# Two-layer attention kernel on one core: four instead of three of the first batch's tiles mixed by ScalarE with TensorE, and the second batch's mixing spread otherwise over GpSimd's queue

## What is computed

```python
x = L0_attn_x                       # [2, 1024, 512]
xn = _layernorm(x)
x = x + attention0(xn) + mix0(xn)   # one head, d = 128; mix0 below
xn = _layernorm(x)
x = x + attention1(xn) + ffn1(xn)   # 32 heads on 8 latent key/value heads, causal; LoRA with top-2 of 8 experts

def mix0(x):                        # a row is seen as 4 streams of 128
    H_res = sinkhorn_log(logits_res, 50)      # 4x4 per row
    H_res = (1 - g) * I + g * H_res
    x_pre = einsum('btnc,btn->btc', x_streams, H_pre)
    y = x_pre @ W_branch
    x_mixed = einsum('btij,btjc->btic', H_res, x_streams)
    return x_mixed + einsum('btc,btn->btnc', y, H_post)
```

## Time and profile before

| what | value |
|---|---|
| median of 3 runs | 2352.6 us (2350.76 to 2353.61) |
| the profiled execution's own time | 2355.71 us |
| its span, first to last instruction | 2353.9 us |
| mean granted TensorE clock | 0.981 of full |
| busy share PE, DVE, ACT, POOL | 95%, 66%, 45%, 43% |
| `layer0_mix` | from about 84.4 to 232.5 us of the span |
| attention of the first batch | from about 352 to 1290 us |

### The profile page before, as it was taken

The page is one execution under the profiler, slowest core; times in us unless marked ns, Lnnn a source line. Parts: engine busy times, 40 slices in busy tenths (PEclk is TensorE's granted clock), DMA queues, the critical chain, the costliest instruction groups (busy, mean ns, idle before and its releaser), DMA issues. The chain is left out here.

```text
span 2353.9 us, 34666 instructions
## 1 busy us (share of the span) xinstructions
PE 2235.7 (95%) x11190; PEld 1817.0 (77%) x11190; DVE 1543.9 (66%) x3818; ACT 1070.3 (45%) x2282; POOL 1017.1 (43%) x1124
## 2 busy tenths in 40 slices
PE   6898999999999999989998898999999999999998
PEld 5554778888888888778777677888888888888886
DVE  6778566777777776746555474656566666666565
ACT  2555334544545454535344232545454545454454
POOL 5331714453536263857654011525344444434341
PEclk9999999999999999999999999999999999999999
DMA  9600582010110101020010464010101010101000
GB/s 339 216 1 17 215 300 81 11 61 27 45 36 36 54 18 54 24 64 24 17 48 6 173 251 152 28 52 20 62 9 62 9 62 9 62 9 62 27 32 32
DMA packets 74168, 165.26 MB, mean 70 GB/s; under 512 B 4721, under 2 KB 38897, under 8 KB 67442
## 3 DMA queue, kind: packets, MB, share of 16 engines
q1 hardware_dynamic: 73650, 162.95, 19.7%
q10 hardware_dynamic: 432, 1.32, 0.1%
HBM read 113.40 MB, written 72.61 MB: 79 GB/s over the span
## 5 line engine op out<-in xcount | busy, mean ns | idle before, releaser
L1868 DVE TENSOR_TENSOR pT<-psum,pT 128x512 fp32r<-128x512 f32 x576 | 387.4, 689 | 265.0 <-ACT pT L1916 262.5
L1768 POOL TENSOR_TENSOR probs_even<-probs_even,rinv 128x1024 f32<-128x1024 f32 (+2 forms) x192 | 241.1, 1256 | 564.0 <-DVE rinv L1859 564.0
L1916 ACT ACTIVATE pT<-psum 128x512 fp32r<-128x512 f32 x576 | 331.5, 597 | 319.3 <-PE psum L1977 319.1
L1854 DVE CUSTOM_DVE_ANT_0 psum<-psum,causal 128x256 f32<-128x256 f32 (+7 forms) x512 | 385.9, 767 | 54.2 <-PE psum L98 50.2
L1907 ACT ACTIVATE probs_even<-psum,nmax 128x1024 f32<-128x1024 f32 (+3 forms) x256 | 204.4, 799 | 263.9 <-DVE nmax L1854 260.5
L1768 POOL TENSOR_TENSOR probs_odd<-probs_odd,rinv 128x896 f32<-128x896 f32 (+2 forms) x192 | 198.8, 1043 | 270.0 <-DVE rinv L1859 269.8
L96 PE MATMUL psum<-keys,q 128*128 128x512 f32 (+3 forms) x768 | 267.9, 349 | 15.3 <-DMA keys<-k_parts 11.6
L97 PE MATMUL psum<-keys,q 128*128 128x512 f32 (+3 forms) x768 | 263.7, 343 | 0.0
L98 PE MATMUL psum<-keys,q 128*128 128x512 f32 (+3 forms) x768 | 263.5, 343 | 0.0
L96 PE MATMUL psum<-pT,vals 128*128 128x512 f32 x576 | 256.4, 445 | 4.5 <-DVE pT L1868 0.7
L1907 ACT ACTIVATE probs_odd<-psum,nmax 128x896 f32<-128x896 f32 (+3 forms) x256 | 176.6, 691 | 146.3 <-DVE nmax L1854 143.5
(11 more groups left out here) (304 smaller groups left out, 4444.6 us busy)
## 6 DMA issues: line engine op xcount, KB each, us to landing
wq<-wq_copy SPq DMA_DIRECT2D x16, 1024.0 KB, 4.8
k_parts<-kv_out SPq DMA_DIRECT2D x32, 512.0 KB, 3.7
v_parts<-kv_out SPq DMA_DIRECT2D x32, 512.0 KB, 3.7
wo<-wo_copy SPq DMA_DIRECT2D x16, 1024.0 KB, 4.8
keys<-k_parts SPq DMA_DIRECT2D x32, 512.0 KB, 4.8
vals<-v_parts SPq DMA_DIRECT2D x64, 256.0 KB, 3.2
acc<-in_x SPq DMA_DIRECT2D x4, 1024.0 KB, 11.8
xn_later<-xn SPq DMA_DIRECT2D x1, 2048.0 KB, 14.5
```

The costliest lines, as they stand in the source:

```text
L1768: pool.tensor_tensor(p, p, rinv[:, u, h:h + 1].to_broadcast([P, (TB - u) * P]), ALU.mult).then_inc(p_ok, 1)
L1854: dve.tensor_tensor_reduce(out=row, in0=row, in1=causal[:, S - n:S], scale=-1.0, scalar=-2 * MASKED, op0=ALU.add, op1=ALU.min, accum_out=n ...
L1868: dve.tensor_tensor(pT[:, n % PT_SLOTS, 1, :], bank[T_BANK + n % 2], f32(pT[:, n % PT_SLOTS, 0, :]), ALU.subtract).then_inc(t_lo, 1)
L1916: act.activation(pT[:, n % PT_SLOTS, 0, :], bank[T_BANK + n % 2], ACT.Copy).then_inc(t_hi, 1)
```

## The change

In `layer0_mix` tile 4 goes from VectorE to the products (15 become 20), and its bias from GpSimd to the bias matmul. The last unit's `branch_in`, `turn_xp`, `branch` and `take_y` go from the attention's loop to the products (behind products 3 and 5 on TensorE, 5 and 7 on ScalarE), in bank 5. The heads' copy `oT` goes ahead of the exponential of the unit's last tile. Nobody waits any more in that stage for the store of y; ScalarE's first write over y's place in `layer1_inputs` and SP's first `later_loads` do. In the first batch's attention the second batch's tiles go 2, 3, 3 instead of 3, 3, 2 to the iterations 5, 6 and 7, with steps per norm of their own for each, and SP's loads of tiles stand at other places. The diff, cut to its core:

```diff
@@ layer0_project, gpsimd
             add_bo(3)
-            add_bo(4)
@@ layer0_mix
-        BY_ACT, SHARE_SLOTS = range(TB - 3, TB), 8
+        BY_ACT, SHARE_SLOTS = range(TB - 4, TB), 8
@@ sync
-            sp.dma_start(m.y_s, y[:, TB:NT, :]).then_inc(later, 16)
-            sp.wait_ge(later, 32)
+            sp.dma_start(m.y_s, y[:, TB:NT, :]).then_inc(m.y_stored, 16)
+            sp.wait_ge(later, 16)
@@ vector
-            for tiles in ((0, 1), (2, 3, 4)):
+            for tiles in ((0, 1), (2, 3)):
@@ scalar (turn_xp, take_y read bank 5 for the last unit)
-                        if qt == 0:
+                        if qt == 0 and unit < UNITS:
                             take_y(unit - 1)
...
+                        if qt == UQ - 1:
+                            act.wait_ge(pv_mm, TB * unit)
+                            act.activation(oT[:], bank[6][:], ACT.Copy).then_inc(o_ok, 1)
                     if unit < UNITS:
                         t = UQ * unit + qt
...
-                if unit:
-                    act.wait_ge(pv_mm, TB * unit)
-                    act.activation(oT[:], bank[6][:], ACT.Copy).then_inc(o_ok, 1)
-                if unit < UNITS:
+                if unit < UNITS - 1:
                     turn_xp(unit)
             for e in range(TB // 2, (NS + 1) * len(BY_ACT)):
                 product(e)
+                if e == TB // 2 + 1:
+                    turn_xp(UNITS - 1)
+                if e == TB // 2 + 3:
+                    take_y(UNITS - 1)
@@ tensor
-                            branch(unit - 1)
+                            if unit < UNITS:
+                                branch(unit - 1)
...
-                if unit < UNITS:
+                if unit < UNITS - 1:
                     branch_in(unit)
...
+                    if e == TB // 2:
+                        branch_in(UNITS - 1)
+                    if e == TB // 2 + 2:
+                        branch(UNITS - 1)
+                    if n == 3 and j == 0:
+                        pe.wait_ge(y_ok, UNITS)
@@ layer1_inputs, scalar
+            if first:
+                act.wait_ge(m.y_stored, 16)
             high_latent(0)
@@ layer1_attention
-            tiles_of = {5: (0, 1, 2), 6: (3, 4, 5), 7: (6, 7)}
-            mixing_steps = {2: (1, 1, 3), 4: (1, 1, 2), 5: (1, 1, 1), 7: (0, 0, 3)}
+            tiles_of = {5: (0, 1), 6: (2, 3, 4), 7: (5, 6, 7)}
+            spread = {0: (1, 1, 1), 2: (1, 1, 1), 4: (1, 1, 1), 5: (1, 1, 1), 7: (0, 0, 3)}
+            mixing_steps = {5: {2: (1, 1, 1), 4: (1, 1, 1), 5: (1, 1, 0), 7: (0, 0, 2)}, 6: spread,
+                            7: {0: (1, 1, 1), 2: (1, 1, 2), 3: (1, 1, 2), 4: (1, 1, 2)}}
@@ sync, loads
-                for t in mixed_now[:2]:
+                for t in mixed_now[:1]:
                     later_loads(t + 1)
...
-                for t in mixed_now[2:]:
+                for t in mixed_now[1:-1]:
                     later_loads(t + 1)
...
                 load(wo[:, 1], m.wo_s[g]).then_inc(wo_in, 16)
+                for t in mixed_now[-1:]:
+                    later_loads(t + 1)
```

More of the change, by code:

```diff
@@ L727, in turn_xp @@
                 act.wait_ge(xp_mm, n + 1)
[L728 removed]
+                act.activation(y[:, UQ * n:UQ * n + UQ, :].rearrange("p t d -> p (t d)"), bank[0 if n < UNITS - 1 else 5][:], ACT.Copy).then_inc(xpT_ok, 1)
             def take_y(n):
                 act.wait_ge(y_mm, n + 1)
[L732 removed]
+                act.activation(y[:, UQ * n:UQ * n + UQ, :].rearrange("p t d -> p (t d)"), bank[1 if n < UNITS - 1 else 5][:], ACT.Copy).then_inc(y_ok, 1)
             def product(e):
@@ L799, in branch_in @@
                     for j in range(NS):
-                        last = pe.matmul(bank[0][:, k * P:(k + 1) * P], shares[:, k, j, :], m.ident[:], start=j == 0, stop=j == NS - 1)
+                        last = pe.matmul(bank[0 if n < UNITS - 1 else 5][:, k * P:(k + 1) * P], shares[:, k, j, :], m.ident[:], start=j == 0, stop=j == NS - 1)
                 last.then_inc(xp_mm, 1)
@@ L805, in branch @@
                 for k in range(UQ):
-                    last = pe.matmul(bank[1][:, k * P:(k + 1) * P], y[:, UQ * n + k, :], wbr[:], start=True, stop=True)
+                    last = pe.matmul(bank[1 if n < UNITS - 1 else 5][:, k * P:(k + 1) * P], y[:, UQ * n + k, :], wbr[:], start=True, stop=True)
                 last.then_inc(y_mm, 1)
@@ L841, in _ @@
                                 pe.wait_ge(w_in, 48)
-                            branch(unit - 1)
+                            if unit < UNITS:
+                                branch(unit - 1)
                             pe.wait_ge(p_exp, UQ * unit)
                             turn(0)
-                            pe.wait_ge(y_ok, unit)
+                            pe.wait_ge(y_ok, min(unit, UNITS - 1))
                             turn(1)
@@ L1712, in _ @@
             if mixes_later:
+                sp.wait_ge(m.y_stored, 16)
                 later_loads(0)
@@ L1716, in _ @@
             if mixes_later:
-                later_loads(TB - 1)
+                for t in tiles_of[ITERS - 1][:-1]:
+                    later_loads(t + 1)
             for u in range(TB):
@@ L1768, in body @@
                         pool.tensor_tensor(p, p, rinv[:, u, h:h + 1].to_broadcast([P, (TB - u) * P]), ALU.mult).then_inc(p_ok, 1)
-                        if mixes_later and it >= mixing_from and u in mixing_steps:
-                            for _ in range(mixing_steps[u][h]):
+                        if mixes_later and it >= mixing_from and u in mixing_steps[it]:
+                            for _ in range(mixing_steps[it][u][h]):
                                 next(beside, None)
@@ L2057, in program @@
         m.xn_s, m.y_s = internal("xn_later", (P, TB, HID)), internal("y_later", (P, TB, D))
-        m.ffn_in, m.ffn_hi, m.copied = (ctx.enter_context(nc.semaphore(n)) for n in ("ffn_in", "ffn_hi", "copied"))
+        m.ffn_in, m.ffn_hi, m.copied, m.y_stored = (ctx.enter_context(nc.semaphore(n)) for n in ("ffn_in", "ffn_hi", "copied", "y_stored"))
         m.w_hi, m.wq_in, m.wq_ok, m.wo_in = ([ctx.enter_context(nc.semaphore(f"{n}{b}")) for b in range(B)]
```

## The result

| kernel | median, us | runs | ratio to before |
|---|---|---|---|
| before | 2352.8 | 4 (2350.8 to 2353.6) | |
| changed | 2328.6 | 4 (2326.8 to 2331.8) | 0.9900 (0.9883 to 0.9917) |
| changed, once more on another chip | 2329.3 | 5 (2326.5 to 2332.4) | 0.9915 (0.9901 to 0.9928), before 2349.3 |

The change makes the kernel 24.2 us faster in the first comparison and 20.0 in the second. The forecast was 2332, by its sum 20.4 less. The ratios are estimated from the executions and are not the quotients of the medians; their intervals reach 2 to 5 us to either side. One execution of the run "changed, copy late" took 3714.8 us at a mean clock of 0.556, a slow state that no other run shows, and its ratio leaves it out.

A forecast was written before the change was run, and what follows sets the result against it. TensorE was taken to bound the attention, losing 30.0 us to late keys and norms in iterations 5 and 6. 2355.7 - 25.7 (attention) + 5.3 (`layer0_mix`) = 2335.3, less 3.1 for the median: about 2332, range 2324 to 2344.

The forecast's parts named there:

- The keys and the norms in iterations 5 and 6: First batch's attention: TensorE's waits for keys and GpSimd's norms, with the half clock behind them, go: -30.0 us before small additions.
- Iteration 6's new stall: First batch's attention: tile 4's data come late, so norm (5, 2) ends after TensorE wants it: 1.4 us lost.
- 0.5 allowed: Iteration 5 of the first batch's attention: no stall in the replay, 0.5 us added for small waits.
- Iteration 7: First batch's attention, 15 steps where 10 were: a tile's handover makes norm (4, 2) late for TensorE, +2.4 us.
- forecast +5.3: `layer0_mix`: the last `oT` is copied sooner, but the longer tail of products moves the end from 232.47 to 237.8.
- ScalarE's chain behind it: `layer0_mix`'s tail: after the last `oT` copy ScalarE waits 9.8 us in `turn_xp`, then products run to 236.0.
- The split of the 7.6 us: `layer0_mix`: last `oT` copied sooner, 5.8 us from the copy's new place, 1.8 from the last unit's `branch_in` and `branch` leaving.
- A: Attention: GpSimd later than replayed, each of five handovers costing 2 us more: +10, 2342 us; chance 0.12.
- B: `layer0_mix` gains a little as ScalarE's wait in `turn_xp` shrinks: -2 instead of +5.3, about 2325 us; chance 0.14.
- C: `layer0_mix`: the sooner heads' copy brings nothing, bank 6's other user limits: +11.1 instead of +5.3, about 2338; chance 0.08.
- D: Attention: the keys stay late or the half clock appears anyway, only norms' waits go: 2353, no change; chance 0.03.
- E: Attention: steps make GpSimd late in all 13 groups of u, 3 us each: +39, 2371 us; chance 0.03.

The follow-up runs named there:

- changed, copy late: The changed kernel with the heads' copy put back behind the exponential of the unit's last tile; 2337.9 us, ratio 0.9950 to before.

## Why the prediction was right

- **The keys and the norms in iterations 5 and 6** (forecast -30.0 + 0.5 + 1.4 = -28.1): measured -28.8. The keys' mechanism is shown by the run that moves SP's one load, the norms' by the run that moves the two steps. What it did not say is how the half clock divides: 4.9 us hung on the keys and 3.8 on the waits for norms.
- **Iteration 6's new stall** at turn (5, 0), forecast 1.4: 1.2. Iteration 5: none, against 0.5 allowed.
- **Iteration 7** (forecast +2.4): the wait is where it was put, 3.79 instead of 2.75. From its first norm to the turn (6, 0) the iteration took 89.2 us in four profiled executions with the old order (89.16 to 89.23) and 94.0 to 95.0 in the five with the new one, so the term was +4.8 to +5.8: twice the forecast or more. The half clock behind the wait was missing in it, though the forecast had counted that for the other waits. Behind that turn both kernels lose another 1.6 us to a fall of the clock in some executions.
- **`layer0_mix`** (forecast +5.3): +5.5 at equal clock in the run of this part alone, +5.9 by its median; +2.7 and +4.7 in the changed kernel's own traces, which had a higher clock at the stage's start. Its steps, with `oT` at 203.15 forecast: 203.59 in the run of this part. ScalarE's chain behind it is right too: from the start of the heads' copy to the end of the last product 32.9 us (200.35 to 233.27), forecast 32.85. The split of the 7.6 us was off, and that their sum came out is luck: the copy alone gives all of it (7.6), while `branch_in` out of the last unit gives 1.8 only if the copy is late (the last `oT` at 208.73 against 210.78 before, 0.3 of it from the start), and nothing beside it.
- **The rivals.** A: GpSimd was later than replayed by 0.6 us at one handover, not by 2 at each of five. The rule of the Trainium skill behind it ("SBUF — State Buffer", section "SBUF: two separate sides") shows in single instructions: three of the 40 products took 1.37, 1.50 and 1.29 where the other 37 took 1.04 to 1.06, and each of the three began while VectorE's own norm (L1882) ran. The other way round, VectorE's norm at 1216.97 took 1.35, begun while a norm of GpSimd's ran, where 14 of the 16 of its shape took 0.55 to 0.86 (rows below the list). GpSimd lost 1.0 us by it in 40 products. No run here had VectorE's part in it apart. B and C are out: the stage costs 5.9 and the copy pays in full. D is out, the keys' wait is zero. E is out: of 13 groups of u with steps two show a wait over 1 us.
- **The sum.** The forecast's 20.4 lies between two errors of like size. The attention gained 23.0 to 23.1 instead of 25.7, as the term for iteration 7 was too small; `layer0_mix` cost 2.7 in the profiled execution instead of 5.3, by a clock that no edit raised. That the total agrees is luck; the other terms are borne out one by one.

For rival A, GpSimd's norm and VectorE's, ahead of the product at 1217.94 (all in the changed kernel):

```profile
1216.72 1.26 POOL L1786 TENSOR_TENSOR probs_odd<-probs_odd,rinv 128x640 f32<-128x640 f32 x1
...
1216.97 1.35 DVE L1882 TENSOR_SCALAR probs_odd<-probs_odd,rinv 128x640 f32<-128x640 f32 x1
```

By the profiled executions the gain was 25.8 us of span. The attention's three iterations give 28.8 - 5.8 = 23.0, `layer0_mix` -2.7, together 20.3. Of the other 5.5, 5.1 lie in stretches whose instructions are nearly the same: 1.6 between `layer0_mix` and the attention, 1.9 between iteration 7 and the second batch's first norm, and 1.6 in the last 20 us (below). These vary as much without the change. The first stretch takes 140.5 us before and 138.8 in the changed kernel, but 137.6 to 139.2 in six other profiled executions with before's instructions there; the second takes 172.0 before, 170.2 in the changed kernel, and 167.9 to 171.8 in the other eleven. At equal clock the edits are worth some 17.5 us (23.0 - 5.5), near the 17.2 that the medians of the two parts add up to.

## What to carry to other kernels

A DMA queue is a program of its own: a load that waits for a slow engine belongs behind the loads that the bound engine needs next, and one moved line there was worth 16 us here (15.9 in the trace, 16.9 by the medians). Work that is to hide beside a bound engine should be laid out in small portions against the times at which that engine wants each result; a replay with a few durations from the trace found each wait within 1.1 us, but a wait that stays costs TensorE's half clock behind it as well. And a change with several edits should be run in parts: here the four tiles by ScalarE, with what goes with them, cost 13 us (+5.5 for the part with them, -7.6 for its copy alone), which the sum hid.

## What the hardware showed

The same idle time of TensorE did not always lower its clock. In `layer0_mix` it waited 1.84 us for slots in five profiled executions with the same instructions there: behind it ten records took 4.74 and 4.75 us in two of them (the changed kernel's first, and the run of this part alone) and 6.98 to 7.09 in three. The last turns of the whole kernel show it too, before and then changed, both with 1.17 idle ahead:

```profile
2333.73 1.23 PE L1977 MATMUL psum<-ident,probs_even 128*128 128x128 f32 x8 [1.17 <-issue]
2334.62 0.78 PE L96 MATMUL psum<-wo,oT 128*128 128x512 f32 x1
2335.19 0.63 PE L97 MATMUL psum<-wo,oT 128*128 128x512 f32 x1
```

```profile
2309.50 1.06 PE L1995 MATMUL psum<-ident,probs_even 128*128 128x128 f32 x8 [1.17 <-issue]
2310.32 0.48 PE L96 MATMUL psum<-wo,oT 128*128 128x512 f32 x1
2310.63 0.39 PE L97 MATMUL psum<-wo,oT 128*128 128x512 f32 x1
```

From that turn's start to the start of the last matmul it takes 16.6 us in five of the thirteen profiled executions, and 15.0 to 15.1 in the other eight, with the same instructions and the same idle time.

The Trainium skill ("TensorE: Matmul & The Clock Gate", section "HAM oscillation — how this bites in real kernels") has idle gaps lower the clock; these rows agree that it happens behind a gap, and show that equal gaps do it in one execution and not in another. Such falls were worth 1.6 to 3 us each, where the changed kernel's four runs spread over 5.0 us; a term of that size can be read from a trace only where the clock is equal on both sides.
